# The kv accumulation of the first tile is moved behind the statistics of the third

## The reference

```python
xn = _layernorm(x)
# attention part (D = 1024)
qkv = xn @ Wqkv + bqkv;  q, k, v = split(qkv)
q = q / norm(q);  k = k / norm(k)
kv = sum(k * v, over the 4096 tokens)       # one vector of 1024 per batch
attn = (q * kv) @ Wout + bout
# FFN (hidden size 4096), ternary weights w and scales s
h = silu(tlin(xn, w1)) * tlin(xn, w2)
h = gelu(tlin(h, h1));  h = gelu(tlin(h, h2))
out = x + attn + tlin(h, w3)
```

## Time and profile before

| | us |
|---|---|
| median of two runs | 3066.9 (3063.35 to 3070.45) |
| the profiled execution | 3056.5 |
| its span on the slowest core, core 4 | 3054.6 |
| the other cores' spans | 3020.0 to 3051.3 |
| TensorE busy, of this span | 2857.7 (94%) |
| VectorE busy | 378.5 (12%) |
| ScalarE busy | 464.6 (15%) |

### The profile page before, as it was taken

How to read it: one execution, slowest core, us unless ns; L and a number is a source line. 1 busy time by engine, 2 the same in 40 slices (tenths; PEclk the granted TensorE clock), 3 DMA queues, 4 the chain that set the end, 5 groups by cost and what they waited for, 6 DMA issues and landing times.

```text
span 3054.6 us, 30463 instructions; the slowest of 8 cores (3020.0 to 3054.6 us)
## 1 busy us (share of the span) xinstructions
PE 2857.7 (94%) x12795; PEld 1280.6 (42%) x13056; DVE 378.5 (12%) x440; ACT 464.6 (15%) x463; POOL 219.9 (7%) x420
## 2 busy tenths in 40 slices
PE   2877899899999999999988899999999999999997
PEld 0333344344444444444433344444444444444443
DVE  3255211432000000000011221100000000000011
ACT  1443211450000000000020031100000000000100
POOL 0000000110000000000000000000000000000000
PEclk8898899999999999999999999999999999999999
DMA  6555444785444444444446554544444444444463
GB/s 153 129 127 130 84 75 77 155 141 90 76 76 76 77 76 77 77 77 77 78 101 133 122 93 70 83 74 77 77 77 76 76 76 76 76 76 76 76 116 91
DMA packets 76598, 278.93 MB, mean 91 GB/s; under 512 B 8752, under 2 KB 8880, under 8 KB 76464
## 3 DMA queue, kind: packets, MB, share of 16 engines
q0 software_dynamic: 59904, 218.13, 43.3%
q1 hardware_dynamic: 16560, 58.85, 6.4%
HBM read 486.66 MB, written 8.39 MB: 162 GB/s over the span
## 4 chain that ended last, share of the span: by engine, by line
PE 83%; DMA 5%; DVE 2%; issue 1%; ACT 1%; SPq 0%; DVEq 0%; ACTq 0%
PE PD L198 23%; PE PC L198 23%; PE PB L198 18%; PE PA L198 18%; DMA xs<-x_fm 4%; DMA out_fm<-os 1%; DVE os L701 1%; DVE os L695 0%; ACT os L667 0%; DVE xb L210 0%; DVE tmp_f L259 0%; ACT Ab L626 0%; DVE Ab L498 0%; DVE Gb L261 0%; SPq L705 0%
## 5 line engine op out<-in xcount | busy, mean ns | idle before, releaser
L198 PE MATMUL PC<-Gb,wr 128*128 128x512 bf16 x2039 | 475.3, 382 | 32.8 <-DVE Gb L261 30.9
L198 PE MATMUL PD<-Gb,wr 128*128 128x512 bf16 x2044 | 473.2, 382 | 2.1 <-issue 0.2
L198 PE MATMUL PB<-Gb,wr 128*128 128x512 bf16 x1687 | 388.7, 380 | 6.1 <-DVE rstd_b L242 4.1
L198 PE MATMUL PD<-Ab,wr 128*128 128x512 bf16 x1503 | 351.8, 385 | 35.5 <-ACT os L667 33.9
L198 PE MATMUL PC<-Ab,wr 128*128 128x512 bf16 x1507 | 345.5, 379 | 3.1 <-ACT os L667 1.3
L198 PE MATMUL PA<-Gb,wr 128*128 128x512 bf16 x1507 | 345.2, 379 | 1.7
L198 PEld LDWEIGHTS PC<-Gb,wr 128*128 128x128 bf16 x2080 | 203.7, 98 | 284.5 <-issue 43.5
L198 PEld LDWEIGHTS PD<-Gb,wr 128*128 128x128 bf16 x2080 | 204.6, 98 | 249.6 <-issue 7.6
L198 PEld LDWEIGHTS PB<-Gb,wr 128*128 128x128 bf16 x1728 | 169.2, 98 | 209.8 <-issue 6.7
L191 POOL DMA_DIRECT2D wr<-h_t x256 | 135.1, 528 | 1616.6 <-PE PB L198 772.9
L198 PEld LDWEIGHTS PD<-Ab,wr 128*128 128x128 bf16 x1536 | 151.7, 99 | 222.4 <-issue 47.1
(11 more groups left out here) (83 smaller groups left out, 1000.3 us busy)
## 6 DMA issues: line engine op xcount, KB each, us to landing
wr<-h_t POOLq DMA_DIRECT2D x256, 512.0 KB, 5.1
xs<-x_fm SPq DMA_DIRECT2D x96, 512.0 KB, 5.1
wr<-w_t POOLq DMA_DIRECT2D x96, 512.0 KB, 5.2
wr<-wqkv_t POOLq DMA_DIRECT2D x56, 512.0 KB, 6.4
out_fm<-os SPq DMA_DIRECT2D x16, 512.0 KB, 3.4
wr<-wout_t POOLq DMA_DIRECT2D x8, 512.0 KB, 7.1
cst<-consts SPq DMA_DIRECT2D x1, 64.0 KB, 1.8
ones_sb<-ones_bf SPq DMA_DIRECT2D x1, 32.0 KB, 3.1
```

The lines of the kernel that those rows point to most:

```text
L198: e.matmul(p[:, h * 512:(h + 1) * 512], l, r, start=a, stop=b),
```

## The change

- For tile 0 the kv work is no longer planned after its V projection. Its arguments are kept, and it is planned in the next iteration, after the statistics of tile 2 and before the xn operations of tile 2, which come after it. The Q projection follows.
- The reciprocal norm of tile 1 gets a buffer of its own, rstdn_c (128 x 1024, F32), and loses the wait for the kv work of tile 0. plan_kv takes the buffer as an argument.
- The kv work of tile 1 stays where it was, and reads rstdn_c.

```diff
+            nc.sbuf_tensor("rstdn_c", [128, TT], F32) as rstdn_c,
         ):
-            def plan_kv(kbuf, vbuf, t_rk, kev, vev):
+            def plan_kv(kbuf, vbuf, t_rk, kev, vev, rbuf):
...
-                    tm = S.op("vector", lambda e, o=oc: e.scalar_tensor_tensor(
-                        prod[:, :], prod[:, :], 1.0, rstdn_b[:, :], ALU.mult, ALU.mult,
+                    tm = S.op("vector", lambda e, o=oc, rb=rbuf: e.scalar_tensor_tensor(
+                        prod[:, :], prod[:, :], 1.0, rb[:, :], ALU.mult, ALU.mult,
...
-                t_rk = plan_norm_rstd("PA", norm_last[0],
-                                      extra=[st["kv_prev_dve"]])
                 if t == 0:
+                    t_rk = plan_norm_rstd("PA", norm_last[0],
+                                          extra=[st["kv_prev_dve"]])
                     plan_stats(1, "PA", "PB")
                 else:
-                    plan_stats(2, "PA", "PB")
+                    t_rk = plan_norm_rstd("PA", norm_last[0], dst=rstdn_c)
+                    emit_xn2 = plan_stats(2, "PA", "PB", defer_xn=True)
+                    plan_kv(*st["kv_args"], rstdn_b)
+                    for _c in range(DC):
+                        emit_xn2(_c)
                 if t == NT1 - 1:
                     plan_qproj(4)
...
-                plan_kv(kbuf, vbuf, t_rk, kev, vev)
+                if t == 0:
+                    st["kv_args"] = (kbuf, vbuf, t_rk, kev, vev)
+                else:
+                    plan_kv(kbuf, vbuf, t_rk, kev, vev, rstdn_c)
```

## The result

The changed kernel is slower: 1.0084 times the kernel before, with a 95% interval of 1.0054 to 1.0115. On 3064.96 us, the median of before over all its runs in that comparison, this is +25.7 us (16.6 to 35.2); the forecast was +25.5. (The plain median of the changed kernel, 3109.89 us, includes executions in which one die ran at a lower clock; the ratio leaves those out on both sides.) The profiled execution took 3080.03 us; 3082.0 had been forecast. Its slowest core is core 6. That the change costs about 25 us is measured; that forecast and median difference agree to 0.2 us is luck, since the interval is 9 us wide on either side.

The account below looks back on a forecast made before the run. The path was taken to run through TensorE, except where it waits for a tile's statistics. Stall 23.5 plus restart 2.0 gave +25.5 us, moving the median 3066.9 to 3092.4 us; range 3078 to 3103.

Parts of the forecast that it names:

- What the removal gives: Taking kv(0) out of 168 to 191.6 us: gain 0, at best 8.7 us, since the third cast waits for ScalarE's Square.
- The order on VectorE: Strictly first-in-first-out queues keep kv(0) out of xn's gaps; without that rule VectorE's chain alone would cost 11 us.
- The stall: Tile 2's Q evacuation waits for the last kv(0) instruction, so TensorE stands still before the norm matmul: +23.5 us.
- The restart: TensorE's first matmuls after the stall run at a lower clock: +2.0 us, bounds 0 and 3.9.
- xn and kv(1): After kv(0), xn ends at about 278.3, 4.7 us before kv(1) needs the first V evacuation: no cost.
- rival B: xn becomes the limit because its x loads meet weight loads: +9 us more, time 3101; chance 0.09.
- The bound of 17.3 us: Lower bound if the Q evacuation need not wait: VectorE's own chain ends kv(1) at 301.9 instead of 284.65.
- Rival A: Only VectorE's chain counts, as the Q evacuation would not wait for deferred kv(0): +17.3 us, 3084.2; chance 0.08.
- The seam: Between the two blocks: VectorE sets the first block's end, so loads and weights shift with it and nothing is absorbed.
- Rival C: The seam gives the time back because x loads land sooner: not slower than before, 3066.9; chance 0.04.
- The low end of the range: Rival A from the lowest run, 3063.35 + 17.3 = 3080.6, less 2.6 us for loads landing sooner: 3078.

Follow-up runs that it names:

- half of kv(0): Changed kernel with chunks 0 to 3 of kv(0) in their old place, only 4 to 7 deferred; second timing 1.0079 of before, first gave no interval.
- kv(0) behind xn: Changed kernel with kv(0) put behind the 16 xn instructions of tile 2; second timing 1.0160 of before, first gave no interval.
- the fastest kernel: Kernel before, with the sums of tile 3's statistics taken chunk by chunk between the V groups of tile 1; ratio 0.9904, -29 us.

## Why the prediction was right

**What the removal gives.** Forecast 0, with 8.7 us as the bound. The first two casts moved to 167 and 170 us and the third stayed with ScalarE's Square; the kernel with only the norm buffer gives 0 too. Right, including its reason.

**The order on VectorE.** The prediction rests it on a rule about the engine's queue. The kernel doesn't need the rule: its scheduler makes every VectorE operation wait for the one before it, so kv(0) could not slip between the xn instructions in any case, and the 11 us that the prediction gives for the other case could not occur. No run here can tell whether the queue alone would have kept the order.

**The stall.** Forecast +23.5 us on core 4. On core 6 of the changed kernel the norm matmul comes 251.74 - 225.74 = 26.0 us after the end of L251; on core 4 of before it was 229.96 - 227.23 = 2.7. Difference: +23.3. TensorE's idle time is 22.29 us there, 22.8 in the mean. Core 4, which was to stay the slowest, was one of the two shortest of the changed kernel (3041.6 us); which core is slowest changes from run to run. Releasers and order are the ones foretold. That the wait is the cause is shown from both sides: with the wait made needless TensorE doesn't stop; with xn (23 to 24 us) in front of it as well, it stops 23 us longer; with half the work, half as long.

**The restart.** Forecast +2.0 us, bounds 0 and 3.9. On core 6 it was 1.01 - 0.59 + 6.13 - 3.62 = 2.9 us. From the norm matmul to the first V evacuation it is 281.03 - 251.74 = 29.3 us, and was 256.36 - 229.96 = 26.4: the same 2.9. But core 6 is one of the two with the dearest restart. Over the eight cores the group took 4.91 to 6.18 us, 5.45 in the mean, so that the restart cost 2.2 us in the mean, and the term is about right in the mean and 0.9 us too low on the core read. Stall and restart together give 23.3 + 2.9 = 26.2 us for this pair of cores. In the mean over the cores it is 24.6. The norm matmul comes 22.7 us later, since cores 0, 1 and 6 of before ran their Q groups more slowly, as worked out for core 1, and so had less to lose; and from it to the first V evacuation it is 1.9 us more (28.6 instead of 26.7).

**xn and kv(1).** Xn was forecast to end 4.7 us before kv(1) needs V. It ended at 274.90, 7.42 us early by the row; kv(1) waits for V as before. Xn took 25.6 us instead of 27.4 (24.8 to 27.5 over the cores, and 27.3 to 29.9 before), so rival B (later loads) had no part, and the sum rightly had nothing for it.

**The bound of 17.3 us** for VectorE's chain alone: measured 14.8 in the mean, and 15.8 on core 4 (300.80 - 227.59 = 73.2, less 57.4). Right in mechanism; xn was again a little quicker than assumed (26.2 us on core 4). Rival A as such didn't occur, since the wait is in force.

**The seam.** Forecast to move as a whole; 44.4 us before and 44.2 after in the mean. Rival C fell. On the two cores compared it was 44.8 and 47.2 us. But the same stretch does give 27 us back when the loads are issued earlier, which its arithmetic (a faster landing) had not had in view.

**The total, and luck.** On core 6 the span is 23.9 us longer than on core 4 of before, where the forecast had 25.5. Its parts are 1.5 us less up to the end of L251, 26.2 more up to the first V evacuation, 2.4 more at the seam and 3.1 less from the first FFN evacuation to the end. Only the second of these was forecast; the others leave 2.2 us by chance. The low end of the range has a slip, too: 8 x 0.3 us is 2.4 and not 2.6, which makes it 3078.2 and changes nothing.

## What to carry to other kernels

Work that is hidden costs nothing where it is; moving it behind the next stage of an in-order engine puts it in front of everything behind it, and what waits for it over a reused buffer can cost more than the engine's own queue, here 24.6 us against 14.8. So before moving work, list who waits for its last instruction, buffers that it only reads included: here K of tile 0 lay in the buffer of Q. And look for the stretch in which the busiest engine really idles: the first casts that the move made early were ready 30 us too soon, while the loads behind the seam, moved into the work ahead of it, gave 29 us.

## What the runs showed of the hardware

A restart of TensorE after a stall of over 10 us costs 1.4 to 3.0 us, and differs more among the cores of one profile than with the length of the stall. In the five profiles with a stall (40 cores) the first two matmuls took 1.01 us each time, where two at full clock take 0.59, and the next group of 16 took 4.58 to 6.18 us instead of 3.62, which makes 1.4 to 3.0 us in all.

| kernel | TensorE idle, mean, us | next group of 16, mean (lowest to highest), us |
|---|---|---|
| half of kv(0), first profile | 11.2 | 5.37 (4.58 to 6.09) |
| half of kv(0), second | 11.1 | 5.28 (4.62 to 6.11) |
| changed | 22.8 | 5.45 (4.91 to 6.18) |
| kv(0) behind xn, first | 46.6 | 5.61 (5.16 to 6.12) |
| kv(0) behind xn, second | 46.1 | 5.53 (5.19 to 5.80) |

The 2.0 us of the row behind 4.23 us of idling, from which the forecast was taken, lie inside this spread. On core 6 of the changed kernel the granted clock is 0.50 (the 1.2 GHz level) from 251.7 to 255 us, right after the stall, and from 259 us on 1.00 (2.4 GHz).

In the fastest kernel the V projection and the FFN follow each other with 1.59 us of idling on every core, behind a stretch in which TensorE was busy only in part. On four cores (1, 2, 4 and 5) the first FFN group then took the full-clock 3.61 or 3.62 us (granted clock 1.00 on core 4); on the others it was slow, 5.30 us on cores 3 and 6 and 6.36 on cores 0 and 7 (granted clock 0.55 on core 0). What decides between them wasn't found.
